# GpSimd waits at the third gather of a chunk until TensorE has transposed the values of the chunk three places back

## The reference

```
x = x + grouped_conv3x3(group_norm(x))              # 8 groups of 64 channels, then a transposition of
                                                    # (channels, pixels) inside each group
h   = relu(bn1(conv1x1(group_norm(x))))             # 512 -> 128 channels
off = conv3x3(h)                                    # 18 channels: (dy, dx) for each of 9 taps
d   = deform_conv3x3(h, off)                        # 128 -> 128 channels
x = x + relu(bn3(conv1x1(bn2(d))))                  # 128 -> 512 channels
```

```
val = v00*wy0*wx0 + v01*wy0*wx1 + v10*wy1*wx0 + v11*wy1*wx1
out = einsum('bckhw,ock->bohw', val, w)             # 9 taps
```

## Time and profile before

| | |
|---|---|
| Time, median of 3 runs | 2210.93 us (2209.67 to 2238.08) |
| The profiled execution | 2238.84 us, its span in the trace 2236.9 us |
| Mean granted TensorE clock | 0.876 of full speed |
| TensorE matmuls busy | 1810.2 us (81%) |
| VectorE busy | 1395.2 us (62%) |
| ScalarE busy | 966.5 us (43%) |
| GpSimd busy | 1182.4 us (53%) |
| DMA queues: gathers, and all others | 45.7% and 13.5% of 16 engines' time |

### The profile page before, as it was taken

The page is one execution under the profiler, slowest core; times in us unless marked ns, Lnnn a source line. Parts: engine busy times, 40 slices in busy tenths (PEclk is TensorE's granted clock), DMA queues, the critical chain, the costliest instruction groups (busy, mean ns, idle before and its releaser), DMA issues.

```text
span 2236.9 us, 31922 instructions
## 1 busy us (share of the span) xinstructions
PE 1810.2 (81%) x10144; PEld 995.9 (45%) x10144; DVE 1395.2 (62%) x3450; ACT 966.5 (43%) x1475; POOL 1182.4 (53%) x1160
## 2 busy tenths in 40 slices
PE   5988787897889788788887888789788878887544
PEld 2544443544545454444444444454444445443221
DVE  5537566574757658466674857668476665846554
ACT  6545353353545435354353545345354443522211
POOL 0046555564556546555564555556455554655664
PEclk9989898897989889888897989899798988988877
DMA  5055665575665656666575665657566575565664
GB/s 181 6 188 154 207 201 179 148 235 173 196 204 169 231 151 219 188 193 194 148 238 164 203 197 181 217 162 238 165 203 199 163 232 156 176 203 160 211 198 154
DMA packets 142933, 412.94 MB, mean 185 GB/s; under 512 B 24614, under 2 KB 25126, under 8 KB 142758
## 3 DMA queue, kind: packets, MB, share of 16 engines
q0 software_dynamic: 92160, 302.06, 45.7%
q1 hardware_dynamic: 50598, 108.71, 13.1%
HBM read 339.37 MB, written 71.30 MB: 184 GB/s over the span
## 4 chain that ended last, share of the span: by engine, by line
PE 47%; DVE 15%; another core or an unknown queue 15%; issue 13%; ACT 5%; POOL 2%; DMA 1%; SPq 1%; ACTq 0%; DVEq 0%; POOLq 0%
PE bank L775 14%; PE bank L757 8%; PE bank L789 8%; DVE sb_rows L567 5%; PE bank L843 4%; PE bank L748 4%; DVE sb_val L575 4%; PE bank L764 3%; PE bank L865 3%; PE bank L808 2%; DVE sb_split L608 2%; POOL sb_rows L332 2%; DVE sb_raw L623 1%; ACT sb_split L406 1%
## 5 line engine op out<-in xcount | busy, mean ns | idle before, releaser
L332 POOL DMA_INDIRECT sb_rows<-table,sb_ridx x1152 | 1178.0, 1023 | 1011.7 <-DVE sb_val L575 440.5
L775 PE MATMUL bank<-sb_split,sb_wg 128*128 128x512 f16 x2304 | 602.5, 409 | 29.6 <-ACT sb_conv_sb L378 20.2
L567 DVE SCALAR_TENSOR_TENSOR sb_rows<-sb_rows,sb_frac 128x256 f32<-128x256 f32 x1152 | 488.3, 479 | 73.6 <-DMA sb_rows<-table,sb_ridx 50.5
L575 DVE SCALAR_TENSOR_TENSOR sb_val<-sb_rows,sb_frac 128x128 f32<-128x128 f32 x1152 | 328.6, 347 | 178.5 <-remote 140.3
L789 PE MATMUL bank<-sb_fold_sb,sb_conv_sb 128*64 128x64 f32 x4096 | 307.1, 287 | 124.6 <-issue 120.3
L775 PEld LDWEIGHTS bank<-sb_split,sb_wg 128*128 128x128 f16 x2304 | 231.2, 104 | 366.3 <-issue 152.9
L616 DVE TENSOR_TENSOR sb_xs<-bank,sb_xs 128x512 f32<-128x512 f32 x128 | 88.3, 690 | 477.4 <-remote 324.6
L757 PE MATMUL bank<-sb_valT,sb_wd 128*128 128x512 f32 x576 | 365.7, 719 | 15.7 <-issue 11.3
L360 ACT ACTIVATE sb_valT<-bank 128x512 f32<-128x512 f32 x288 | 171.2, 595 | 407.5 <-remote 249.1
L789 PEld LDWEIGHTS bank<-sb_fold_sb,sb_conv_sb 128*64 128x64 f32 x4096 | 271.0, 206 | 166.9 <-issue 161.1
L378 ACT ACTIVATE sb_conv_sb<-bank,sb_bias 128x512 f32<-128x512 f32 x256 | 173.6, 685 | 387.7 <-PE bank L775 219.2
(11 more groups left out here) (77 smaller groups left out, 1095.3 us busy)
## 6 DMA issues: line engine op xcount, KB each, us to landing
table<-sb_table_sb SPq DMA_DIRECT2D x144, 256.0 KB
sb_xs<-x SPq DMA_DIRECT2D x64, 512.0 KB
out<-sb_res SPq DMA_DIRECT2D x128, 256.0 KB
sb_rows<-table,sb_ridx POOLq DMA_INDIRECT x1152
sb_rows<-w_group SPq DMA_DIRECT2D x8, 288.0 KB, 9.3
sb_wd<-w_def SPq DMA_DIRECT2D x1, 576.0 KB
sb_w<-w_in SPq DMA_DIRECT2D x1, 256.0 KB
sb_w<-w_out SPq DMA_DIRECT2D x1, 256.0 KB
```

What stands on the lines that cost most here:

```text
L332: pool.indirect_dma_start(out=rows[:, (c % RING) * PER + i, :], out_offset=None, in_=tables[u % 2], in_offset=bass.IndirectOffsetOnAxis(ap ...
L567: op = nc.vector.scalar_tensor_tensor(r[:, 0:2 * CH], r[:, 2 * CH:4 * CH], frac[:, parity, half * PER + i, k, 0:1], r[:, 0:2 * CH], ALU.mu ...
L575: op = nc.vector.scalar_tensor_tensor(val[:, c % 2, i * CH:(i + 1) * CH], r[:, CH:2 * CH], frac[:, parity, half * PER + i, k, 1:2], r[:, 0 ...
L775: op = nc.tensor.matmul(pair_ps[half][:, :], wg[:, g, k, :], plane(split1[:, g, :], ky + half * HROWS, kx, HROWS), start=k == 0, stop=k == ...
```

## The change

GpSimd issues the first two gathers of a chunk as before. Before the third it waits until TensorE has transposed the values of the chunk three places back, the chunk whose place in `rows` this one takes. For chunk c of image t that is `valT_done` >= 18 t + c - 2. The `sem_inc` on `pool_passed` goes with each wait of this program. Nothing else changes: the same gathers, in the same order, to the same places.

```
                     pool.wait_ge(val_done, count(CHUNKS, t, c - RING + 1))
                     pool.sem_inc(pool_passed, 1)
                     for i in range(PER):
+                        if i == 2:
+                            pool.wait_ge(valT_done, count(CHUNKS, t, c - 2))
+                            pool.sem_inc(pool_passed, 1)
                         pool.indirect_dma_start(
                             out=rows[:, (c % RING) * PER + i, :], out_offset=None, in_=tables[u % 2],
```

## The result

Four executions each, on one chip: the changed kernel took 2080.93 us in the median (2064.44 to 2095.71), the kernel before 2216.48 us (2209.67 to 2238.08). The ratio of the medians is 0.939. The forecast was 2050 us, within 1950 to 2220; the sign, the mechanism's place and the range held, and the gain came out at 136 us between the medians where 161 was forecast. The profiled execution of the changed kernel, 2095.71 us, is the slowest of its four; its span is 2093.9 us against 2236.9 before, 143.0 us less.

The account below looks back on a forecast made before the run. TensorE's late work beside long gather runs was taken as the bound, at most 469 us. 13 us an image times 14 images is 182 us, 126 at the lower end; 162 was taken, giving 2050 us, range 1950 to 2220.

Parts of the forecast that it names:

- What bounds the kernel: VectorE's and ScalarE's "remote" waits are for late TensorE work: at most 469 us, 27.2% of the chain from 250 to 1975 us.
- no change: Rival: something other than runs slows TensorE, or the number of gathers does; 2211 us (2190 to 2230), chance 0.20.
- the rule: Trainium skill's statement that a DMA never contends with a compute engine; by it the time would stay at 2211 us.
- A pause ends it.: Long gather runs make TensorE's slow state likely and a pause ends it; two runs of four, 0.68 us apart, had no stall.
- None begins before the run is four gathers old: In the image walked through, no long ScalarE wait for TensorE starts before four gathers of the run are out.
- The walk through image 7: Gains at five long runs of one image, 2.4 + 4 + 3.5 + 2.5 + 5.3 = 17.7 us, less 4, called 13.
- what comes back: Held gathers join the next image's first eight, one more run that can stall: 4 us an image taken off.
- The cost of the instructions: The 288 added waits with sem_inc on GpSimd: 0 to 0.3 us each, taken as 0; image 15 at most 5 us.
- Late gathers: Rival: held gathers reach VectorE late, at chunk 16; 3 us an image, 45 us, 2256 us in all, chance 0.08.
- Nearly all stalls go: Rival: cut runs never stall and the clock stays up; up to 28 us an image, about 1850 us, chance 0.07.
- The signs: Trace changes listed beforehand as right (such as "remote" waits down a third, image starts 120 us apart) or wrong.
- The scaling: Profiled execution from 2238.8 to 2057 us, scaled by 0.919 to a median of 2031; with 162 us taken, 2050.

Follow-up runs that it names:

- m1: Bench of its own, groups of nine matmuls beside gathers or plain copies: 65.5 us beside 24 back-to-back gathers, 44.7 us in every other stage.
- m3: Bench with m1's matmuls, varying rows, number and spacing of gathers, and signals: 46.8 us undisturbed, 47.5 at 1.44 us a gather, 70.1 beside 24 in one run.
- stage (4): Part of m3: 216 matmuls with a single signal at the end, beside 24 gathers: 64.4 us, against 46.8 us alone.
- e3: Kernel before plus a fixed pause of 1.22 us ahead of each chunk's first gather, no hold: 2015.57 us, 0.902.
- e9: e3 repeated on another chip: 2022.82 us, 0.881.
- m2: Bench with m1's matmuls beside 24 gathers spaced in seven ways: 65.3 us in one run, 44.7 us in runs of four with 1.24 us gaps.
- m4: Bench with one engine at a time beside 24 gathers, then alone: TensorE's small matmuls 185.2 us against 170.9, ScalarE's copies 32.35 against 31.26.
- e7: e3 with the pause before every second chunk only: 2202.36 us, 0.964.
- e1: Changed kernel with the hold at each chunk's first gather instead of the third: 2079.8 us, 0.930.

## Why the prediction came out as it did

**What bounds the kernel.** Right, and shown: long "remote" waits are TensorE's work come late beside dense gathers. In m1, as in the kernel from 1169.26 and from 2147.73, the matmuls begin on time and their signals come late; in m3's stage (4), as in the shuffle of the earlier trace rows, the matmuls begin late as well. With gathers thinned out the kernel is 10 to 12% faster (e3, e9). The rival "no change" is out by m1, and with it the use that it made of the rule.

**"A pause ends it."** This is the step that was wrong. The reading took runs of five and more as the cause and 0.68 us as enough to reset them, from two runs of four without a stall. By m2 and m3 the average spacing decides, with about 1 us of excess allowed where each nine matmuls have a signal. The two runs of four were widely spaced; their first and last gather, kernel before:

```profile
1144.89 1.29 POOL L332 DMA_INDIRECT sb_rows<-table,sb_ridx  x1 [6.98 <-DVE sb_val L575]
...
1155.07 1.00 POOL L332 DMA_INDIRECT sb_rows<-table,sb_ridx  x1 [0.30 <-issue]
```

Eight gathers in 10.18 us are 1.45 apart, without any excess, so the 0.68 us of pause need not have done anything. "None begins before the run is four gathers old" holds under either reading, which is why the trace could not tell them apart. One exception fits as well: the run of 8 from 1110.49, which has no stall, is spaced at 1.43 us, and the two runs of 8 that have one at 1.26 and 1.31. The other does not: in image 15 the 13 gathers from 2111.32 to 2127.05 are 1.31 apart, 1.7 us of excess by then, and TensorE still answers at once; it has little work there, and late onsets (after 14 gathers) are seen in m3 and m4 too. What slows single gathers in the kernel is not shown; m4 shows that VectorE can hold one.

**The walk through image 7.** The places were right; the sum was too large. It gave 17.7 - 4, which is 13.7 and was called 13, times 14 images, and after the deduction 162 us; spread over the fifteen periods measured that is 10.8 us each, and 9.4 were measured. The mis-sized term is the one for what comes back. A hold releases two gathers at once and the next chunk's follow at 1.25 us, so after each hold a new run forms: at the image's start the full 6.63 us was still there (2.4 us had been counted off), the run from 1045.72 was held after twelve and its wait was 5.09 us instead of 6.61 (2.5 had been counted). The mean run fell from 9.2 to 6.2 gathers, but runs of eight and more only from 84 to 66. By the rate rule the hold could not do much more: GpSimd still issues at 1.25 us whenever it issues, and only standing idle in between lowers the rate (1.34 us before in dense stretches, 1.36 after). Two terms that the sum put at nothing pull in opposite ways. The clock gave up to 3.4 us an image, so what the cut stalls gave by themselves may be as little as 6 of the 9.4. Against it, VectorE waits 2.3 us an image more for gathers (line 570). The runs don't price either on the chain.

**The cost of the instructions.** Taken as 0, with 5 us for image 15. Image 15 gave 1.9 us net, where 5 gained and 5 lost were expected. Fits, within what one trace can tell.

**Rivals on the other side.** "Late gathers" came true in part: VectorE's waits for gathers at line 570 are 82.9 us in the whole run, 3.8 at most, against 50.5 before. In images 2, 5 and 12 they grew by about 4 us each and in image 14 by 8.3, but what TensorE gained outweighed them. "Nearly all stalls go" did not happen, for the reason that the prediction gave: where TensorE keeps up, ten and twelve gathers go out unheld. e3, where nearly all of them go, came to 2016 us and not to the 1850 that it priced, since with the pause GpSimd's own 6.2 us a chunk is the next bound; a kernel without stalls and without that bound is not among the runs.

**The signs.** Waits by line 751 on GpSimd: there, 98, with less idle time in total, as forecast. Long waits end before chunk 17 is out: yes (1085.21 against 1107.27, its fourth gather). First gathers 120 us apart: 123.0. "Remote" waits down by a third or more: not quite; at the three lines named they fell from 714 to 518 us, 27%, as they did in all. Share of the unknown queue down: no, the same per image. The mean wait went from 5.8 to 5.0 us and the number from 179 to 153, so stalls were shortened more than they were prevented. Line 570 waiting in the middle images, which was a sign of being wrong: yes, somewhat, 3.5 us an image instead of 1.3.

**The scaling.** The profiled spans differ by 143.0 us, the medians by 135.6; the forecast's 161 is too large by 18 to 25 us. The runs that formed again are the term for it that the trace shows; the clock and the later gathers, put at nothing, are in it with either sign.

**What stays open.** Why TensorE stands. The matmuls begin at multiples of 0.70 us with nothing to wait for, the loss goes with the number of gathers and not with bytes or rows, plain copies from the same queue don't cause it, and it is small for 48 wide matmuls and for ScalarE's 60 copies, but large for matmuls that begin often. That would fit a shared supply that both GpSimd's making of gathers and TensorE's instructions draw on, but it remains a guess, and one form of it the traces speak against: TensorE does not wait for a transfer of instructions. In m1 such transfers, of 16 KB, mostly come every 24 to 30 us; none begins between 48.04 and 98.01, though TensorE stood for most of the time from 66 to 86 us, and that gap is longer than the others by about what the stall cost. A rival without a test is the recording itself, which also grows with the number of instructions and not with their size: every execution of the changed kernel and of the experiments has a recorded span and clock, so none is known to have run without it. e7's gain is open too.

## What to carry to other kernels

A wait that is put down to an unknown source, on a kernel that has one core, is worth laying beside the other engines' queues before a cause is chosen; then vary the suspected cause alone, in a kernel that holds nothing else. Where indirect gathers run beside TensorE, look at their spacing: here a fixed pause that made it 1.54 us on average (e3, 0.902) beat a hold that answers only to TensorE's delay (e1, 0.930 on the same chip). Before two sums of waits are compared, take out the engine that the change itself makes wait, and compare traces of one chip. Two readings that agree on every row of a trace, as run length and rate did here, need a stage of their own before one of them carries a sum.

## What the runs showed of the hardware that I had not expected

- 24 back-to-back indirect gathers, 1.25 us apart, made 216 matmuls of 512 columns, with a signal for each nine, take 65.5 us instead of 44.7, with no data in common, and a signal came up to 20 us after its matmul had begun; plain copies from GpSimd 0.61 us apart, and from SyncE, did nothing (m1).
- In the benches the threshold lies between 1.44 us a gather (0.7 us lost over 24, m3) and 1.46 (nothing lost, m2). The first late group comes after five or six gathers at 1.25 us (m1); with no signals between the matmuls the first late one comes after 14 (m3, m4). 128 KB and 64 rows count like 256 KB and 128 rows.
- During a stall matmuls begin at multiples of 0.70 us (m3, m4).
- 72 VectorE instructions with two inputs in SBUF, back to back, held one gather for 25.82 us (m4).
- The kernel before took 2216, 2236, 2291 and 2295 us in four comparisons, the last three on three chips, while e3's pattern took 2016 and 2023 on two of these: the ratio of the same kernel came out as 0.902 and 0.881.
